# First attention: TensorE's order inside a unit written out by hand, search tiles given out 15 ahead instead of 12

## What is computed

```
xn = layernorm(x);  q, k, v = xn@wq, xn@wk, xn@wv      16 heads of width 8, 2 batches
scores = q @ k.T    per head, 1024 x 1024
out = softmax(scores / sqrt(128)) @ v + xn
```

## Time and profile before

| what | us |
|---|---|
| median of three timed runs | 1112.01 |
| profiled execution, whole | 1116.44 |
| its span | 1114.7 |
| units 2 to 29 of the first attention (78.03 to 413.33) | 335.30 |
| one of these 28 units | 11.975 |
| unit 30, the last with searches in it (413.33 to 423.89) | 10.56 |
| unit 0, at the low TensorE clock (52.20 to 66.06) | 13.86 |

### The profile page before, as it was taken

One profiled execution on the slowest core, in us unless ns is written; L12 is line 12 of the kernel. 1 busy time (PEld: TensorE's weight loads), 2 busy tenths in 40 slices (PEclk: granted clock), 3 DMA queues, 4 the chain that ended last, 5 costly groups with the idle time before them and its releaser, 6 DMA issues. The chain is left out here.

```text
span 1114.7 us, 16176 instructions
## 1 busy us (share of the span) xinstructions
PE 969.4 (87%) x5608; PEld 549.5 (49%) x5608; DVE 728.9 (65%) x1443; ACT 629.0 (56%) x1253; POOL 331.9 (30%) x361
## 2 busy tenths in 40 slices
PE   4698888888988985887589999999999999578998
PEld 2222222222222222522467676767677676466997
DVE  6888888888888883424645454545454554565776
ACT  3267777777777775322345546555565554344665
POOL 4600000000000000000665748493756740221222
PEclk9689999999999998689789999999999999797999
DMA  3320000000000001000000000000000000200000
GB/s 66 142 91 15 22 17 15 21 17 15 20 18 16 20 4 24 4 0 14 1 1 10 1 4 4 10 1 6 11 1 1 5 2 1 77 1 1 11 16 15
DMA packets 22745, 20.02 MB, mean 18 GB/s; under 512 B 5064, under 2 KB 17328, under 8 KB 22664
## 3 DMA queue, kind: packets, MB, share of 16 engines
q1 hardware_dynamic: 22664, 18.99, 5.8%
HBM read 14.26 MB, written 4.59 MB: 17 GB/s over the span
## 5 line engine op out<-in xcount | busy, mean ns | idle before, releaser
L400 DVE TENSOR_REDUCE halves<-max_bank 128x2 f32<-128x1024 f32 x256 | 309.9, 1224 | 40.8 <-PE max_bank L542 32.9
L509 ACT ACTIVATE probs<-score_bank 128x512 f32<-128x512 f32 x512 | 267.5, 602 | 108.6 <-PE score_bank L580 108.5
L1390 PE MATMUL a_sum<-a_turned,a_v 128*128 128x512 f32 (+3 forms) x384 | 158.5, 500 | 0.8 <-ACT a_headsT L1319 0.6
L1145 ACT ACTIVATE a_probs<-a_scores,a_lowest 128x896 f32<-128x896 f32 (+7 forms) x128 | 94.9, 741 | 112.4 <-DVE a_lowest L1140 111.9
L580 PE MATMUL score_bank<-q_stack,k_stack 50*128 50x512 bf16 x512 | 133.8, 392 | 27.4 <-ACT probs L509 24.6
L593 PE MATMUL summed<-probs,v_tile 128*32 128x512 f32 x1024 | 138.1, 612 | 0.2 <-ACT probs L509 0.2
L542 PE MATMUL max_bank<-k_stack,q_stack 48*128 48x512 bf16 x512 | 115.2, 393 | 19.4 <-DVE halves L400 19.2
L580 PEld LDWEIGHTS score_bank<-q_stack,k_stack 50*128 50x128 bf16 x512 | 33.7, 93 | 187.0 <-ACT probs L509 141.0
L1140 DVE TENSOR_REDUCE a_lowest<-a_scores 128x1 f32<-128x896 f32 (+7 forms) x128 | 96.2, 755 | 40.6 <-PE a_scores L1134 40.1
L338 POOL COPY v_tile<-values 128x128 f32<-128x128 f32 x16 | 4.7, 296 | 338.8 <-PE summed L593 338.1
L1381 PE MATMUL a_turn<-identity,a_probs 128*128 128x128 f32 x576 | 96.4, 277 | 4.9 <-ACT a_probs L1145 4.9
(11 more groups left out here) (260 smaller groups left out, 1585.9 us busy)
## 6 DMA issues: line engine op xcount, KB each, us to landing
rope<-in_rope SPq DMA_DIRECT2D x1, 2048.0 KB, 8.0
m_w<-in_L_ffn_mlp_w SPq DMA_DIRECT2D x8, 256.0 KB, 4.5
q_parts<-l_q_parts SPq DMA_DIRECT2D x2, 768.0 KB, 4.9
k_parts<-l_k_parts SPq DMA_DIRECT2D x2, 768.0 KB, 6.3
q_stack<-q_parts SPq DMA_DIRECT2D x30, 48.0 KB
k_stack<-k_parts SPq DMA_DIRECT2D x30, 48.0 KB
x<-in_L_attn_x SPq DMA_DIRECT2D x2, 512.0 KB, 4.1
q_stack<-shift SPq DMA_DIRECT2D x64, 2.0 KB
```

The costliest lines, as they stand in the source:

```text
L400: dve.reduce_max(halves[:, u % 2, half, :].rearrange("p (x t) -> p x t", x=2)[:, :, qt], max_bank[place % RING][:, :, :], AX_X).then_inc(f ...
L509: act.activation(probs[:, k % PROBS, x, :], score_bank[e % SCORES][:, :], ACT.Exp, scale=SCALE0).then_inc(prob_ready, 1)
L1145: act.activation(probs[:, k % 2, c, 0:row_width(n)], scores[n % 2][:, 0:row_width(n)], ACT.Exp, bias=lowest[:, n % 8:n % 8 + 1], accum_out ...
L1390: pe.matmul(sum_bank[:, skipped(k, j):CH], v[:, BLOCKS[k][0], j, :], turned[:, m % SLOTS, skipped(k, j):CH], start=(j == 0), stop=(TURNED_ ...
```

## The change

`LEAD` becomes 15. The loop over steps is replaced by `unit_of(u)`, which writes out one unit: scores are given one, two or three at a time, ring places (`next_place`) stand between them, and the value steps keep their numbers but stand at other places of the ring. The ring of a unit is now five searches, turn, search, fold, two searches; before it was five searches, turn, two searches, fold, search. ScalarE's loop is written over one counter instead of two and does the same in the same order. SyncE's and GpSimd's programs are not edited.

```
-LEAD = TILES + 4
-FOLD_AT = 6
+LEAD = 2 * TILES - 1
...
+RING_OF_UNIT = ("search",) * 5 + ("turn", "search", "fold", "search", "search")
...
+                    next_scores(1)
+                    next_place()
+                    next_scores(2)
+                    next_place()
+                    next_scores(1)
+                    if u >= 1:
+                        use(u - 1, GROUPS - 1)
+                    next_scores(1)
+                    next_place()
+                    next_scores(1)
+                    next_place()
+                    next_scores(2)
+                    use(u, 0)
+                    next_place()
+                    next_scores(3)
+                    next_place()
+                    use(u, 1)
+                    next_place()
+                    next_scores(2)
+                    next_place()
+                    next_scores(1)
+                    next_place()
+                    next_scores(2)
+                    next_place()
+                    use(u, 2)
...
                 for u in range(UNITS0):
-                    for k in range(TB):
-                        for x in range(2):
-                            score(u, k, x)
-                        for event in ring_of_step(u, k):
-                            give_ring(event)
-                        if k == 1 and u >= 1:
-                            use(u - 1, GROUPS - 1)
-                        if k % 2 == 1 and k >= 3:
-                            use(u, (k - 3) // 2)
+                    unit_of(u)
```

More of the change, by code:

```diff
@@ L124, with ring_of_unit @@
 VALUE = HD0 + 1
[L127 to L135, removed]
+RING_OF_UNIT = ("search",) * 5 + ("turn", "search", "fold", "search", "search")
+def ring_of_unit(u):
+    m = TILES * u + LEAD
+    for what in RING_OF_UNIT:
+        if what == "search":
+            yield ("search", m) if m < TILES * UNITS0 else None
+            m += 1
+        if what == "turn":
+            yield ("turn", u + 1) if u + 1 < UNITS0 else None
+        if what == "fold":
+            yield ("fold", u - 1) if u >= 1 else None
 def ring_before():
@@ L147, in ring_uses @@
     for u in range(UNITS0):
-        for k in range(TB):
-            yield from ring_of_step(u, k)
+        yield from filter(None, ring_of_unit(u))
     yield "fold", UNITS0 - 1
@@ L499, in _ @@
                 mid(7)
[L501 to L505, removed]
-                        for x in range(2):
-                            e = 2 * (u * TB + k) + x
-                            act.wait_ge(score_ready, e + 1)
-                            act.activation(probs[:, k % PROBS, x, :], score_bank[e % SCORES][:, :], ACT.Exp, scale=SCALE0).then_inc(prob_ready, 1)
-                        if k == 1 and u >= 1:
-                            take(u - 1)
+                for step in range(UNITS0 * TB):
+                    u, k = divmod(step, TB)
+                    if step >= PROBS and step % 2 == 0:
+                        done = (step - PROBS) // 2 + 1
+                        act.wait_ge(used, done)
+                    for x in range(2):
+                        e = 2 * step + x
+                        act.wait_ge(score_ready, e + 1)
+                        act.activation(probs[:, step % PROBS, x, :], score_bank[e % SCORES][:, :], ACT.Exp, scale=SCALE0).then_inc(prob_ready, 1)
+                    if k == 1 and u >= 1:
+                        take(u - 1)
                 take(UNITS0 - 1)
@@ L569, in give_ring, with score @@
                         fold_heads(n, place)
-                def score(u, k, x):
+                def score(e):
+                    step, x = divmod(e, 2)
+                    u, k = divmod(step, TB)
                     pair, half = divmod(u, 2)
-                    rows, e = slice(x * ROW, x * ROW + NST + 2), 2 * (u * TB + k) + x
+                    rows = slice(x * ROW, x * ROW + NST + 2)
                     if k == 0 and x == 0:
                         pe.wait_ge(shift_in[u % 2], 32 * (u // 2 + 1))
-                    if u == 0 and k == 0:
+                    if e == 0:
                         pe.wait_ge(v_out, NCH)
@@ L595, in use, with unit_of, next_scores, next_place @@
                     last.then_inc(used, 1)
+                def unit_of(u):
+                    scores = iter(range(2 * TB * u, 2 * TB * (u + 1)))
+                    ring = ring_of_unit(u)
+                    def next_scores(count):
+                        for _ in range(count):
+                            score(next(scores))
+                    def next_place():
+                        event = next(ring)
+                        if event is not None:
+                            give_ring(event)
+                    next_scores(1)
[23 more added lines that the diff above has]
+                    use(u, 2)
                 pe.wait_ge(w_in, 16 * NW)
```

## The result

The changed kernel takes **1136.14 us** (median of four runs, 1133.46 to 1137.00); beside it the kernel before took 1114.28 (1110.85 to 1116.76). The ratio is 1.0194, with an interval of 1.0156 to 1.0233: slower by 22 us. The forecast was 1127 within 1107 to 1138. Its range holds the time and its sign is right; the loss of 15 us was too small.

The account below looks back on a forecast made before the run. VectorE has the most to do, 10.4 us of an 11.975 us unit, the rest mostly waits for late search tiles. Terms -36.8 - 0.9 + 0.4 + 40.6 + 12 = +15 gave 1127 us, range 1107 to 1138.

Parts of the forecast that it names:

- the clock: TensorE's granted clock falls to 0.50 at 9 or 10 of 14 load stalls, 1.3 us each: +12, bounds 0 and +21.
- The order inside the unit: Reordered scores, searches and value steps in each unit: 10.70 us instead of 11.975, -36.8 over units 1 to 29.
- The term of -37.7 with unit 30: The new order's gain: -36.8 in units 1 to 29 and -0.9 in unit 30, which has fewer searches left.
- three waits of 0.31: VectorE's waits for a late search tile, three a unit of 0.31 us, claimed to vanish with the new order.
- 0.28 us of the join: In VectorE's unit, the join was counted as 0.28 us of the 10.4 us a never-waiting unit takes.
- single scores: In TensorE's order, a search stands behind one score, not two; named first for the waits of 0.31 being gone.
- The three tiles ahead of the first unit: Three more tiles on VectorE before the first score, mostly hidden by the shift DMA: +0.4, bounds 0 and +1.5.
- The load of the next pair: Second search of even units waits for its load; TensorE stands 2.93 us, 2.9 us lost for each of 14 pairs: +40.6.
- two of three: Clock falls at two of three earlier pauses of similar length, taken as the rate for the 14 stalls: 9 or 10.
- The third rival: Clock falls at nearly every stall and the next value step is hit too: +21 or more, 1136 to 1142; 10%.
- the loads might be in time: Rival 1: next pair's tile finds its data when VectorE needs it, so only the order counts: 1075; 7%.
- The wait without the clock: Rival 2: the load wait as reckoned while TensorE's clock stays high: +3, 1115 us; 18%.

Follow-up runs that it names:

- the kernel with the order alone: The changed kernel with LEAD back at 12, so only the new order inside the unit: 1076.06 us, ratio 0.9681.
- the loads first: The changed kernel, LEAD 15 kept, with load_head ahead of subtract(u + 1) in SyncE's loop: 1074.28 us, ratio 0.9671.
- The halves: Two kernels with LEAD 12 and one half of the unit in the new order: first half new 1098.89 us, second half new 1074.95 us.
- the old order with LEAD 15: The kernel before with LEAD 15 alone, turn and fold at their old places: 1176.40 us, ratio 1.0606.
- the pause filled: The changed kernel with ten pairs of thrown-away search matmuls ahead of TensorE's wait for the load: 1113.07 us, ratio 1.0017.
- LEAD 14: The changed kernel with LEAD = 2 * TILES - 2 instead of 15: 1092.16 us, ratio 0.9811.
- LEAD 13: The changed kernel with LEAD = 2 * TILES - 3 instead of 15: 1079.98 us, ratio 0.9707.

## Why the prediction was right, and where it was off

The mechanism is the predicted one, term by term; one term of the sum, the clock, was mis-sized, beyond its own upper bound of 21 us. Over the stage the clock cost 14 us more than summed, wait and order together came out 4 us better, and the later layers gave back 4.4 us that no term speaks of. Without these 4.4 us the time would be over 1138, so that the range holds it is in part luck.

**The order inside the unit.** Stepped: 10.70 us a unit, 11.94 for before. Measured: 10.67 in odd units, 10.68 in the kernel with the order alone, 11.975 before. The term of -37.7 with unit 30 measures -37.5 in units 2 to 30 (335.30 + 10.56 before, 298.75 + 9.65 with the loads first); the -40.1 by the stage ends has units 0, 1 and 31 in it too. The reason given holds in the main: the three waits of 0.31 are gone, though with the loads first one of 0.2 us a unit is left, behind the split. The near agreement hides two errors of 0.1 to 0.2 us that cancel: the 0.28 us of the join was no cost of the join but a late tile (0.09 where the tile is ready), and the reduction behind the split comes that much later behind it. The halves show that the value step that left the fold's neighbourhood and the places in the second half carry most of it, while the text named the single scores first.

**The three tiles ahead of the first unit.** Stepped +0.4; the first score stands at 52.64 instead of 52.20. That proves nothing: it stands at 52.22 and 52.07 in two other kernels with a lead of 15, and at 51.64 and 51.85 in two with 12.

**The load of the next pair.** The split ends 7.39 us into an odd unit, stepped 7.50. The load is seen 7.33 us behind the split in the mean (6.8 to 7.7), stepped 7.2, and 0.6 us behind the last transfer, as taken from the earlier trace rows. The search comes 2.90 us late where 2.93 was stepped; the 3.2 of the view is the idle time, which the prediction put at 3.2 as well. Worth 40.6 by the sum, 40.5 by the units, 39.1 by the stage ends. The Trainium skill's fixed cost of about 2.0 us for a DMA (DMA: Bandwidth & Descriptors, "Anatomy of one DMA"), weighed there as 8 us less, was not borne out: from the start of its issue to the search that waits for it the last load took 2.8 us in the mean. That section of the page is on DMAs issued from GpSimd, and these are issued by SyncE.

**The clock.** This is the term that was mis-sized: +12 in the sum, 23 to 26 measured. Both factors were too low. Falls: 9.5 taken, 13 counted. Price of one: 1.3 taken, 23.0 / 13 = 1.8 measured (2.0 by the stage ends). The step behind the price that failed is that the low clock lasts no longer than the 3.3 us for which it had been seen. For six falls that held (3.4 us, with one slow value step), and their price was 1.1 in the mean, close to the 1.3. Behind the other seven (105.84 to 112.5 above is one) it lasted 6.8 us, met a second value step each time and cost 2.3. The trace of before had both numbers. The windows of the earlier trace rows are only 3.3 us wide; the one that begins at 563.10 goes on at the low clock:

```profile
566.50:569.80 3.30, 3.30 (x15) 0.50 0.00 0
1023.90:1027.20 3.30, 2.88 (x13) 0.50 0.00 0
```

The second row is the window at a fourth pause of this length, 3.38 us, which the prediction leaves out: three of four fell, not two of three. The third rival, with a price of +21 or more, 1136 to 1142, came true with a chance of 10%. That the pauses would let the clock fall, and that next to nothing hides it behind a stall, was right.

The Trainium skill (TensorE: Matmul & The Clock Gate, "Terms") prices a low clock at half of the time spent in it. The granted clock over units 2 to 29 is in this row of the changed kernel:

```profile
77.21:439.52 362.31, 309.60 (x2044) 88.65 (x2045) 290.83 (x365) 251.41 (x476) 4.10 (x14) 0.91 0.05 16
```

A mean of 0.91 means 18% of 362.31, some 65 us, at 0.50. The page's rule gives an estimate of 33 us; measured were 23 to 26. In the old order with LEAD 15 ten falls with 113 us at 0.50 cost 35 to 38 us, where the rule would give 56. So half of the low time is too much here; that the missing part lay in slack of TensorE is likely, but not shown.

**The rivals.** That the loads might be in time (7%) is refuted for this kernel, but its time of 1075 was the right one for the kernel in which they are: 1074.28 and 1076.06 were measured. The wait without the clock was put at 1115 and measured at 1113.07 with the pause filled. So the sum's other terms stand, and the miss of 7 us is the clock's 14, less what order, wait and later layers gave back.

**Still open:** why the clock returns after 3.4 us in some units and after 27 us with the old order, TensorE being busy in both, and why it fell at four of the pauses with LEAD 14 and none with LEAD 13. The length of the pause alone does not decide it: it fell at one of 1.0 us (LEAD 14) and not at ones of 1.5 (LEAD 13), 2.1 (old order) and 2.8 (the changed kernel). The runs show that it happens and what it costs, not by what rule.

## What to carry to other kernels

When a consumer is moved earlier, follow its operands back to the queue that issues their loads: here three tiles more of lead made a load late that had been 2.6 us early by the stepping, and a reordered issue on SyncE gave it all back. A wait of TensorE costs more than its length if the clock falls at it. How often it falls has to be counted: here at 13 of 14 pauses of 2.3 to 3.6 us, 10 of 14 of 1.2 to 2.1 us (old order), 4 of 14 of 0.6 to 1.7 us (LEAD 14) and none of 14 of 0.4 to 1.5 us (LEAD 13). How long it stays low is read from stretches of the profile up to the point where it is back, not from one of fixed length. Filling the pause with matmuls that are thrown away is a cheap way to measure that part.

## What the runs showed that was not expected

- A pause of 1.70 us was enough to let the clock fall, and it then stayed at 0.50 for 27 us while TensorE was drawn busy 97% of the time. In the old order 10 falls cost 35 to 38 us, in the new order 13 falls cost 23 to 26. Whether it is the order that brings the clock back sooner was not tested.
- The later layers, the same instructions in all kernels, took 666 to 677 us, with the granted clock at 0.93 to 0.95. A change of the first stage by 7 us can vanish in that.
- VectorE can start the reduction 0.09 us behind the join when its tile is ready (102.25 to 102.34), not the 0.28 of the rows of before.
